# A graph layer's output pass: weights from Sigmoid instead of Relu, clamp and Exp, and two features kept in DRAM

## The reference

```
h = relu(layernorm(x));  de = diag(adj);  A = adj with zero diagonal
for head k: hW = h @ W[k]
    e_plus, e_minus = leaky_relu([hp, hm] @ a[k]), leaky_relu([hm, hp] @ a[k])
    att[i, j] = e_plus[j] if A[i, j] > 0, e_minus[j] if A[i, j] < 0, else -9e15
    support += softmax(att, axis=1) * A @ hW
node_output = gru(support / 3, h);  edge_output = gru(A @ h, h)
x = x + de * edge_output + de * node_output
```

## Time and profile before

| | |
|---|---|
| median of 3 runs | 2103.26 us (2102.48 to 2103.84) |
| profiled execution | 2101.93 us, its span 2100.1 us |
| busy: TensorE, VectorE, ScalarE | 1875.6 (89%), 1663.2 (79%), 1469.0 (70%) |
| norm pass, first to last matmul of L1711 | 1220.2 to 1339.4 us |
| output pass, first to last matmul of L1749 | 1345.19 to 2077.97 us |
| behind it to the end of the span | 22 us |

### The profile page before, as it was taken

The page is one execution under the profiler, slowest core; times in us unless marked ns, Lnnn a source line. Parts: engine busy times, 40 slices in busy tenths (PEclk is TensorE's granted clock), DMA queues, the critical chain, the costliest instruction groups (busy, mean ns, idle before and its releaser), DMA issues.

```text
span 2100.1 us, 22007 instructions
## 1 busy us (share of the span) xinstructions
PE 1875.6 (89%) x7997; PEld 1195.3 (57%) x7997; DVE 1663.2 (79%) x2462; ACT 1469.0 (70%) x1453; POOL 13.4 (1%) x15
## 2 busy tenths in 40 slices
PE   2335999789998989989999989899999999999997
PEld 1223888578877989965555556444444444444443
DVE  4658989698877888887878762698889888988985
ACT  3445666456668999988777631597878878887873
POOL 0000000000010000000000000000000000000000
PEclk9999999899999999999999999999999999999999
DMA  9999899588885777669999698443232323423220
GB/s 389 429 428 378 324 343 344 192 292 317 318 314 185 250 247 248 249 229 360 350 336 357 247 338 288 136 135 130 86 110 105 112 104 115 132 97 117 105 75 11
DMA packets 81563, 489.51 MB, mean 233 GB/s; under 512 B 8449, under 2 KB 12546, under 8 KB 36402
## 3 DMA queue, kind: packets, MB, share of 16 engines
q1 hardware_dynamic: 77138, 485.94, 62.8%
q10 hardware_dynamic: 4320, 2.20, 0.4%
HBM read 452.36 MB, written 35.75 MB: 232 GB/s over the span
## 4 chain that ended last, share of the span: by engine, by line
PE 63%; DVE 16%; ACT 10%; DMA 7%; issue 3%; SPq 0%; DVEq 0%; ACTq 0%
PE bank L1749 26%; DMA ring<-in_adj_rows 7%; PE bank L1551 5%; PE bank L1711 5%; PE bank L1553 5%; PE bank L1552 5%; ACT work L630 4%; DVE work L1395 3%; ACT work L625 3%; PE bank L1625 2%; DVE a_lo L982 2%; DVE reg L1395 1%; PE bank L1654 1%; PE bank L1630 1%; PE bank L1631 1%
## 5 line engine op out<-in xcount | busy, mean ns | idle before, releaser
L1749 PE MATMUL bank<-work,reg 128*128 128x512 f32 x960 | 422.5, 595 | 17.3 <-DVE ring L1344 11.4
L1395 DVE TENSOR_TENSOR work<-work,ring 128x1536 f32<-128x1536 f32 x160 | 280.3, 1752 | 68.0 <-ACT work L803 67.1
L1749 PEld LDWEIGHTS bank<-work,reg 128*128 128x128 f32 x960 | 181.8, 191 | 246.2 <-issue 220.2
L982 DVE TENSOR_TENSOR a_lo<-ring,a_hi 128x2048 fp32r<-128x2048 f32 x128 | 292.5, 2301 | 31.0 <-ACT a_hi L574 30.1
L574 ACT ACTIVATE a_hi<-ring 128x2048 fp32r<-128x2048 f32 x128 | 244.2, 1912 | 76.3 <-PE bank L1553 76.3
L1585 PE MATMUL bank<-reg,ring 128*128 128x129 f32 x2048 | 242.6, 281 | 27.6 <-DVE ring L1096 27.4
L1585 PEld LDWEIGHTS bank<-reg,ring 128*128 128x128 f32 x2048 | 238.0, 197 | 31.5 <-DVE ring L1096 20.7
L803 ACT ACTIVATE work<-work 128x1536 f32<-128x1536 f32 x160 | 235.3, 1471 | 26.1 <-DVE work L1373 26.1
L1749 PE MATMUL bank<-reg 128*128 128x512 f32 x576 | 252.4, 592 | 0.0
L1551 PE MATMUL bank<-a_hi,s_hi 128*128 128x512 f32 x512 | 206.8, 404 | 21.2 <-DVE a_lo L982 21.2
L1553 PE MATMUL bank<-a_hi,s_lo 128*128 128x512 f32 x512 | 201.6, 394 | 0.0
(11 more groups left out here) (235 smaller groups left out, 2649.4 us busy)
## 6 DMA issues: line engine op xcount, KB each, us to landing
ring<-in_adj_units SPq DMA_DIRECT2D x320, 1024.0 KB, 4.9
ring<-in_adj_rows SPq DMA_DIRECT2D x32, 2048.0 KB, 17.0
ring<-masks SPq DMA_DIRECT2D x64, 512.0 KB, 4.6
masks<-work SPq DMA_DIRECT2D x48, 512.0 KB, 9.2
masks<-ring SPq DMA_DIRECT2D x16, 512.0 KB, 9.2
reg<-lines SPq DMA_DIRECT2D x8, 768.0 KB, 10.3
ring<-lines SPq DMA_DIRECT2D x8, 768.0 KB, 7.9
out<-ring ACTq DMA_DIRECT2D x8, 256.0 KB, 2.3
```

Of the source, the lines that this page charges most:

```text
L982: dve.tensor_tensor(a_lo[:, ring_at(p, g)], ring[:, ring_at(p, g)], a_hi[:, (g % 4) * UNIT:(g % 4 + 1) * UNIT].bitcast(F32), ALU.subtract) ...
L1395: dve.tensor_tensor(tv, tv, spread(ring[:, ring_at("out", g, q * W, W)], HEADS, 1), ALU.mult).then_inc(s_y, 1)
L1749: last = pe.matmul(bank[1 + k][:, :], h, tiles(c * T + t)[:, k * W:(k + 1) * W], start=t == 0, stop=t == T - 1)
```

## The change

- Weights: ScalarE computes sigmoid(e - guard) for each head, three activations of 512 columns a tile, with the guard 20 higher (`MARGIN`) and the reciprocal sums smaller by exp(-20). The clamps, Relus, and Exp go. The product with the adjacency stays one instruction of 1536 columns. VectorE has no clamp in the pass; where entries are negative (`arguments`) it prepares the arguments.
- Buffers for tiles: seven instead of eight, in `work`, `reg2` and the end of the ring. Guards lie in `x`; tables `vp` and `vm` lie in `work`.
- `x` and h turned are stored to DRAM during the norm pass (between mask loads 19 and 20, and 27 and 28, in SyncE's queue), and come back in pieces of 256 KB for each chunk (`load_chunk`).
- TensorE's last two tiles of a chunk go head by head, and `take_chunk` and `heads` wait for each head by itself (`s_head`).
- Behind the last chunk the gate matmuls on h are issued before or between `heads` and the source, and the reset gate goes first.
- One more small VectorE step in `norm_nodes_in`.

```diff
-GROUPS = 8
+TILES = 7
 AHEAD = 2
...
+MARGIN = 20.0
...
+        def tile_of(n, plain, reg, tail):
+
+            b = n % TILES
+            if b < 5:
+                return plain[:, b * THREE:(b + 1) * THREE]
+            return reg[:, 0:THREE] if b == 5 else tail[:, 13 * W:13 * W + THREE]
 
         def tiles(n):
 
-            b = n % GROUPS
-            size = HEADS * W
-            if b < 5:
-                return work[:, b * size:(b + 1) * size]
-            if b < 7:
-                return reg3[:, (b - 5) * size:(b - 4) * size]
-            return reg4[:, 2 * size:3 * size]
+            return tile_of(n, work, reg2, spare)
...
         def guards_at(c):
 
-            return reg4[:, (c % 2) * HEADS * W:(c % 2 + 1) * HEADS * W]
+            return x[:, (c % 2) * THREE:(c % 2 + 1) * THREE]
 
         def guard(c, k):
             return guards_at(c)[:, k * W:(k + 1) * W]
 
-        def on_act(t):
-
-            return 2 if t % 2 else 1
-
-        nmask = reg3[:, 6 * W:7 * W]
-        slow = reg3[:, 7 * W:8 * W]
-        spare = ring[:, RING_OUT * UNIT:G * UNIT]
-        rden = spare[:, 0:HEADS * W]
+        x_chunk, h_chunk = (x[:, 2 * THREE + i * W:2 * THREE + (i + 1) * W] for i in range(2))
+        nmask = work[:, 5 * THREE:5 * THREE + W]
+        guard_copy = [reg2[:, 2 * THREE:2 * THREE + W], reg2[:, 2 * THREE + W:2 * THREE + 2 * W], reg4[:, N:N + W]]
+        rden = spare[:, 0:THREE]
         nk = spare[:, 3 * W:6 * W]
         n_temps = [spare[:, (6 + i) * W:(7 + i) * W] for i in range(6)]
         res = spare[:, 12 * W:13 * W]
+
+        def cell_state(p, c):
+
+            return reg2[:, at(c, W, -W, W)] if p == "edge" else h_chunk
...
+        def tile_used(n):
+
+            c, t = n // T, n % T
+            return (s_head, HEADS * (c + 1)) if t == T - 1 else (s_used, c * (T - 1) + t + 1)
...
-                    sp.wait_ge(s_clamp, (c - 1) * T)
-                    sp.wait_ge(s_relu, (c - 1) * T)
+                    sp.wait_ge(s_exp, (c - 1) * T)
+                else:
+                    sp.wait_ge(s_xs, 16)
                 spread(0, c, guards_at(c)).then_inc(s_guards[c % 2], 16)
 
             def load_dens(c):
@@ -447,17 +464,36 @@
                     sp.wait_ge(s_mm["norm"], G * C)
                 spread(HEADS, c, rden).then_inc(s_dens, 16)
 
+            def load_chunk(c):
+
+                if c > 1:
+                    sp.wait_ge(s_res["out"], c - 1)
+                else:
+                    sp.wait_ge(s_xs, 16)
+                    sp.wait_ge(s_hs, 16)
+                sp.dma_start(x_chunk, xs_d[:, (c - 1) * W:c * W]).then_inc(s_xload, 16)
+                sp.dma_start(h_chunk, hs_d[:, (c - 1) * W:c * W]).then_inc(s_hload, 16)
+
             for n in range(MASKS, C * G):
+                if n == 20:
+                    sp.wait_ge(s_gv["edge"], C * CELL_STEPS)
+                    sp.dma_start(hs_d, reg2[:, :]).then_inc(s_hs, 16)
+                if n == 28:
+                    sp.wait_ge(s_res["edge"], C)
+                    sp.dma_start(xs_d, x[:, :]).then_inc(s_xs, 16)
                 load_masks(n)
             load_guards(0)
             load_guards(1)
             for n in range(RING_OUT, C * G):
                 load("out", n)
+                if n > G and n % G == 2:
+                    load_chunk(n // G)
                 if n % G == 6:
                     c = n // G
                     load_dens(c)
                     if c and c + 1 < C:
                         load_guards(c + 1)
+            load_chunk(C)
...
-            def first_clamps(n):
+            def weights(n):
 
                 c, t = n // T, n % T
                 if t == 0:
                     act.wait_ge(*guards_loaded(c))
-                if n >= GROUPS:
-                    act.wait_ge(s_used, n + 1 - GROUPS)
-                elif n >= 5:
+                if n >= TILES:
+                    act.wait_ge(*tile_used(n - TILES))
+                elif n >= AHEAD:
                     act.wait_ge(s_mm["norm"], G * C)
-                for k in range(on_act(t)):
-                    last = act.activation(tiles(n)[:, k * W:(k + 1) * W], guard(c, k), ACT.Relu,
-                                          bias=(ne0, ne1)[k][:, t:t + 1])
-                last.then_inc(s_relu, 1)
-
-            first_clamps(0)
+                    act.wait_ge(s_hs, 16)
+                act.wait_ge(s_arg, n + 1)
+                for k in range(HEADS):
+                    last = act.activation(tiles(n)[:, k * W:(k + 1) * W], guard(c, k), ACT.Sigmoid,
+                                          bias=e6[:, t * SCORES + k:t * SCORES + k + 1], scale=-1.0)
+                last.then_inc(s_exp, 1)
+
+            for n in range(AHEAD):
+                weights(n)
             for c in range(C):
                 for t in range(T):
                     n = c * T + t
@@ -796,13 +835,14 @@
                         candidate("out", c)
                     if c and t == 29:
                         store(c)
-                    if n + 1 < C * T:
-                        first_clamps(n + 1)
-                    act.wait_ge(s_clamp, n + 1)
-                    act.wait_ge(s_relu, n + 1)
-                    act.activation(tiles(n), tiles(n), ACT.Exp, scale=-1.0).then_inc(s_exp, 1)
+                    if n + AHEAD < C * T:
+                        weights(n + AHEAD)
             keep_edge_support(C)
-            gates("out", C)
+            act.wait_ge(s_lastg, 1)
+            act.wait_ge(s_gv["out"], (C - 1) * CELL_STEPS)
+            act.activation(n_temps[1], bank[5][:, :], ACT.Tanh, bias=gb[:, 4:5], scale=0.5).then_inc(s_lastr, 1)
+            act.wait_ge(s_gm["out"], C)
+            act.activation(n_temps[2], bank[6][:, :], ACT.Tanh, bias=gb[:, 5:6], scale=0.5).then_inc(s_ga["out"], 1)
             candidate("out", C)
...
+                if p == "out" and c == C:
+                    dve.wait_ge(s_lastr, 1)
+                    dve.wait_ge(s_lastg, 2)
+                else:
+                    dve.wait_ge(s_ga[p], c * 2 - 1)
...
+                if p == "out":
+                    dve.wait_ge(s_hload, 16 * c)
+                s.link(dve.tensor_tensor(gr, cell_state(p, c), gn, ALU.subtract))
...
-                    xq = x[:, at(c, W, q * P - W, P)]
+                    xq = x[:, at(c, W, q * P - W, P)] if p == "edge" else x_chunk[:, q * P:(q + 1) * P]
...
-                s.link(dve.tensor_scalar(g_at(3), g_at(1).bitcast(I32), LN2 / 2 ** 23, 0.1 - 127 * LN2,
+                s.link(dve.tensor_scalar(g_at(3), g_at(1).bitcast(I32), LN2 / 2 ** 23, 0.1 + MARGIN - 127 * LN2,
                                          ALU.mult, ALU.add))
                 s.link(dve.tensor_tensor(g_at(6), g_at(2), g_at(3), ALU.add))
-                s.inc(dve.tensor_tensor(g_at(4), g_at(2), g_at(6), ALU.subtract))
+                s.link(dve.tensor_tensor(g_at(4), g_at(2), g_at(6), ALU.subtract))
+                s.inc(dve.tensor_scalar(g_at(4), g_at(4), MARGIN, None, ALU.add))
...
-                dve.wait_ge(s_used, c * T)
                 dve.wait_ge(s_dens, 16 * c)
                 if c > 1:
                     dve.wait_ge(s_es, c - 1)
                 for k in range(HEADS):
+                    dve.wait_ge(s_head, HEADS * (c - 1) + k + 1)
                     dve.tensor_tensor(nk[:, k * W:(k + 1) * W], bank[1 + k][:, :],
                                       rden[:, k * W:(k + 1) * W], ALU.mult).then_inc(s_nk, 1)
 
-            def clamps(n, negatives):
+            def arguments(n):
 
                 c, t = n // T, n % T
+                s = Steps(dve, s_slow, SLOW_STEPS, n)
+                if n:
+                    dve.wait_ge(s_exp, n)
                 if t == 0:
                     dve.wait_ge(*guards_loaded(c))
-                if n >= GROUPS:
-                    dve.wait_ge(s_used, n + 1 - GROUPS)
-                elif n >= 5:
-                    dve.wait_ge(s_mm["norm"], G * C)
-                s = Steps(dve, s_slow, SLOW_STEPS, n)
-                if negatives:
-
                     if n == 0:
                         dve.wait_ge(s_mm["norm"], G * C)
-                    dve.wait_ge(*loaded("out", c, t // Q))
-                    if n:
-                        dve.wait_ge(s_clamp, n)
-                    dve.wait_ge(s_relu, n + 1)
-                    s.link(dve.tensor_scalar(nmask, ring[:, ring_at("out", t // Q, (t % Q) * W, W)],
-                                             0.0, None, ALU.is_lt))
-                for k in range(0 if negatives else on_act(t), HEADS):
-                    arg = guard(c, k)
-                    if negatives:
-                        s.link(dve.scalar_tensor_tensor(slow, nmask, d_e[:, t * HEADS + k:t * HEADS + k + 1],
-                                                        arg, ALU.mult, ALU.add))
-                        arg = slow
-                    last = dve.tensor_scalar(tiles(n)[:, k * W:(k + 1) * W], arg,
```

(64 more changed lines are left out.)

33 lines of the change are left out of this document (22 added, 11 removed).

## The result

The median of the changed kernel is 2087.0 us (2085.33 to 2087.95, 4 runs) against 2102.87 for the kernel before: ratio 0.9923, 95% interval 0.9906 to 0.9940. It is 15.9 us faster. The forecast was 2086.0, range 2081 to 2096. The profiled execution took 2087.61 us, with a span of 2085.8.

The account below looks back on a forecast made before the run. TensorE was taken to bound the output pass, so its idle moments count. Boundaries -13.2, start -0.1, tail -5.2 and stores +1.2 sum to -17.3 us: 2084.6 us profiled, 2086.0 us on the median, range 2081 to 2096.

Parts of the forecast that it names:

- The bound: Output pass: TensorE bounds it, so work taken off ScalarE and VectorE hides under it and gains nothing directly.
- the rival on the other side: Output pass: Sigmoid is slow and ScalarE becomes the bound; at twice the Relu price 2370 us; chance 0.04.
- Boundaries, -13.2: Seven chunk boundaries of the output pass: TensorE's 11.4 us of waits and 0.25 us refill behind each go, -13.2 us.
- the step's 0.98 us: Chunk boundaries with lighter VectorE but old order: expected loss of 0.63 plus 0.1 wait and 0.25 refill per chunk.
- The start, -0.1: Start of the output pass: a 1.283 us table load replaces the first Exp of 1.47 us, -0.1 us.
- The clock term: Start of the output pass: a shorter wait could return up to 2 us of slow TensorE clock; none counted.
- The tail, -5.2: Behind TensorE's last tile: the chain to the last result shrinks from 19.4 to 14.2 us, gain 5.2, range 4 to 6.
- The stores, +1.2: Norm pass: two 2.10 MB stores delay backlogged mask loads, costing TensorE 1.2 us; bounds 0 and +7.8.
- Two equal stalls: Norm pass, units 20 and 28: the stores' cost appears as mask-load waits of about 0.6 us each.
- The sum: Whole kernel: -13.2 - 0.1 - 5.2 + 1.2 = -17.3 us, from 2101.93 to 2084.6 us profiled, 2086.0 as median.

Follow-up runs that it names:

- experiment 2: Kernel before, keeping Relu, clamps and Exp, with the last two tiles of each chunk and the products by the sums head by head: 2099.03 us, ratio 0.9977.
- experiment 6: Changed kernel with as many VectorE clamps as before, written to unused memory: 2098.93 us, ratio 0.9974.
- experiment 1: Changed kernel with the last two tiles of a chunk in the old order and products by the sums waiting for all three heads: 2095.53 us, ratio 0.9957.
- experiment 7: Changed kernel with a one-column Sigmoid before the last guard rows of the norm pass, loading the table early: 2085.05 us, ratio 0.9913.
- experiment 3: Changed kernel with the old tail: behind the last chunk heads, all six gate matmuls, then both tanh: 2089.3 us, ratio 0.9931.
- experiment 8: Changed kernel with six unread matmuls keeping TensorE busy between the norm and output passes: 2085.31 us, ratio 0.9917.
- experiment 4: Changed kernel with the two stores moved to mask loads 36 and 48 instead of 20 and 28: 2084.03 us, ratio 0.9913.
- experiment 5: Changed kernel with h stored twice, back to back, in front of mask load 20: 2092.13 us, ratio 0.9943.
- experiment 10: Changed kernel with stores at loads 36 and 48, early table load, first four tiles by head, two matmuls in the gap between passes: 2078.88 us, ratio 0.9875.

## Why the prediction was right

**The bound.** Right: less work on ScalarE and VectorE gave nothing directly, and everything at the places where TensorE stood still. ScalarE's Sigmoid, the one price that no row had, came out at the nearest row, 0.71 us alone and 0.62 in a row, so the rival on the other side fell, and with it most of the risk.

**Boundaries, -13.2.** Right in size and in mechanism. The waits of 11.4 us and the refills went; the chunk is 90.56 us where 90.58 was worked out. The output pass shrank by 12.4 although its start got 0.9 us slower (13.44 against 12.52 for the first 24 records), so the boundaries gave 13.3. The steps behind it hold too: VectorE reaches `take_chunk` before head 0 ends (1.13 us before; I had said about at the same time), and either half alone falls short. Order alone gives 92.61 and 92.67 us a chunk (experiments 2 and 6), light VectorE alone 91.78 (experiment 1), against the 91.56 that the step's 0.98 us makes. One detail was not seen: the first of the seven waits, 0.79 us, came from the order alone, since VectorE was not late there (experiment 2). The sum took all seven as measured, so it is none the worse for that.

**The start, -0.1.** Right: 5.84 to 5.81 us. The load took 1.28 us with the copy ending right in front of it, and moving it away gave 1.4 (experiment 7). On the Trainium skill's price (ScalarE: Activation LUTs, "What ACT_TABLE_LOAD costs"), about 2.66 us for load and drain, the trace disagrees: no drain is visible in front of or behind the load, and the measurement decides. The clock term, counted at nothing, was 0.9 us against the change in that execution, and 0.5 for it in the other (12.02 against 12.52).

**The tail, -5.2.** Right, step for step: from TensorE's last tile `cell_in` was to run from 7.1 to 9.1 us and ran from 7.0 to 9.0. The chain is 14.2 us in the second execution of the changed kernel, as worked out, and 13.7 in the first. The 0.5 between them is the last turn, 1.13 or 0.67 us, at granted clock 0.50 or near 1; the prediction took it at 1.13 and did not name the clock there. How the gain divides I had wrong in the expectations of experiments 2 and 3: the third product costs nothing even without a gate matmul in front of `heads`, since `heads` waits head by head and the product lies under its own first two matmuls. So the products head by head give 2.2 us (1.2 expected), the gate order 3.0 (4.5 expected).

**The stores, +1.2.** Right in place, and in size within the scatter: 1.9 us behind the stores in one execution of the changed kernel, 0.5 in the other, and in the seven profiles with the stores at these places (experiments 1, 3, 6, 7 and 8 too) 0.5 to 2.4 us, 1.6 in the mean. Two equal stalls were expected; they were 0.3 and 1.6 us, and 0.5 and nothing. Bytes over the rate of the saturated stretch (410 GB/s taken, 408 measured over 29 us of backlog) was a sound way to price an unmeasured transfer. Moved out of the backlog the stores cost nothing (experiment 4); one more inside it lengthened the wait by 4.6 to 4.8 us, near the transfer's own 5.1 (experiment 5).

**The sum.** -17.3 was forecast; the medians differ by 15.9, and the two profiled executions by 14.3, 3.0 less than forecast. Of these, 2.0 us lie ahead of the norm pass, in passes that the change leaves alone, where it varies by as much between executions of the same code. What sets it is open; no experiment was made on it. The norm pass gave 0.6 less than forecast and the output pass 0.8, which is the slower clock at the start; the start itself lacks the 0.1, and the tail gave 0.5 more. The mechanism carries the forecast, but that the median came within 1.0 us of it is in part chance: the passes ahead, the clock at the start, the clock at the last turn and the waits at the stores each move by 0.5 to 2.4 us from execution to execution.

## What to carry to other kernels

When one engine is busy 98% of a stage, price a change by its idle moments and follow the chain back from each: here nine products after a late turn decided a wait that the list names by a quite different instruction. A gap with two causes in a row, a late engine and an order that lets nothing overlap, pays less than half if only the first is removed (0.82 of 2.04 us), and nothing if only the second is, except where the engine was not late. Put extra transfers where the queue has no backlog: the same bytes cost nothing sixteen to twenty units later. And read a short tail in more than one execution: one of its steps here took 0.67 or 1.13 us with the same code.

## What the runs showed of the hardware

Six matmuls whose results nobody reads, put into 5.8 us of idleness, kept the granted clock at 1.00 (2.4 GHz) in every 5 us stretch of the start: 10.57 us for 24 records. Without them the granted clock over the first 5 us of the pass was 0.50 (1.2 GHz throughout) in the profile of the changed kernel, 0.70 in its second and 0.60 in the kernel before, and the 24 records took 12.0 to 13.6 us. An idle time of 4.4 us was still enough for the fall (experiment 7, 13.63 us), and one of 5.1 us in the norm pass too (experiment 5); behind the wait of 1.6 us in the norm pass the clock stayed at 1.00, and with 2.1 us, mostly filled, it did not fall either (experiment 10).

The last turn stands behind 4.1 us in which TensorE does nothing. In ten profiles with that gap it took 0.67 us in four and 1.13 in six, with the same code and a granted clock near 1 or of 0.50. In the three profiles with a gap of 6.2 us (before, experiments 2 and 3) it took 1.13 each time.

A table load takes 1.28 us. At the start of the pass it begins 0.01 us after the copy ends, and the Sigmoid begins 0.02 us behind it. Tanh needed no load after Sigmoid, and none after Exp in the kernel before.

Mask loads of 512 KB and a store of 2 MB share the DMA engines at 408 GB/s, the rate of the loads alone (410).
